# Linear attention with a routed feed-forward on one Trainium2 core: product groups of the attention loop run in pairs, with other PSUM banks

## What is computed

```python
xn = _layernorm(x)
qkv = xn @ W_qkv.T                                   # q, k, v by head
q_p = elu(einsum('bhnd,hdf->bhnf', q, proj)) + 1.0
k_p = elu(einsum('bhnd,hdf->bhnf', k, proj)) + 1.0
kv = einsum('bhnf,bhnd->bhfd', k_p, v)
attn = einsum('bhnf,bhfd->bhnd', q_p, kv)
z = 1.0 / (einsum('bhnf,bhf->bhn', q_p, k_p.sum(axis=2)) + 1e-08)
attn = (attn * z[..., None]) @ W_out.T + b_out
weights = softmax(where(logits >= second_best, logits, -inf))   # logits = xn @ Wr + br
ffn = sum over e of weights[e] * (gelu(xn @ W1[e] + b1[e]) @ W2[e] + b2[e])
out = x + attn + ffn
```

## Time and profile before

| | |
|---|---|
| median of 3 runs | 706.27 us (706.25 to 707.19) |
| profiled execution | 706.3 us |
| its span, first to last instruction | 704.2 us |
| TensorE, share of the span busy | 97% |
| VectorE, ScalarE | 73%, 68% |
| mean granted TensorE clock | 0.997 of full speed |
| HBM traffic | 94 GB/s over the span |

### The profile page before, as it was taken

How to read it: one execution, slowest core, us unless ns; L and a number is a source line. 1 busy time by engine, 2 the same in 40 slices (tenths; PEclk the granted TensorE clock), 3 DMA queues, 4 the chain that set the end, 5 groups by cost and what they waited for, 6 DMA issues and landing times.

```text
span 704.2 us, 17250 instructions
## 1 busy us (share of the span) xinstructions
PE 682.1 (97%) x5482; PEld 600.8 (85%) x5483; DVE 511.3 (73%) x1308; ACT 476.1 (68%) x875; POOL 227.5 (32%) x169
## 2 busy tenths in 40 slices
PE   8799999999999998999999999999999999999995
PEld 4666777777777776589999999999999999999995
DVE  8889989898989878847567674556776445577553
ACT  5687969696969696776477764457774444777551
POOL 1313232323242324633252332234223323313222
PEclk9999999999999999999999999999999999999998
DMA  8866474747474648856365563345636333554431
GB/s 262 197 183 169 108 226 105 226 106 226 106 226 105 196 105 230 232 169 187 58 105 170 80 165 46 52 65 93 188 60 171 51 47 67 87 150 60 58 46 22
DMA packets 87204, 91.63 MB, mean 130 GB/s; under 512 B 60049, under 2 KB 73361, under 8 KB 84897
## 3 DMA queue, kind: packets, MB, share of 16 engines
q1 hardware_dynamic: 71426, 59.36, 34.1%
q0 software_dynamic: 13872, 18.75, 15.2%
q10 hardware_dynamic: 1872, 13.11, 5.0%
HBM read 39.32 MB, written 26.67 MB: 94 GB/s over the span
## 4 chain that ended last, share of the span: by engine, by line
PE 79%; DVE 8%; issue 4%; SPq 3%; DMA 3%; ACT 2%; POOL 1%; POOLq 0%; DVEq 0%
PE F L502 9%; PE F L503 9%; PE F L504 9%; PE WK L502 5%; PE WK L504 4%; PE WK L503 4%; PE NUM L502 4%; PE NUM L504 4%; PE NUM L503 4%; PE DEN L574 4%; PE DEN L503 3%; PE DEN L502 3%; PE DEN L504 3%; PE F L565 3%; PE F L559 3%
## 5 line engine op out<-in xcount | busy, mean ns | idle before, releaser
L1864 POOL DMA_INDIRECT out<-ysb,icur x75 | 120.3, 1604 | 273.2 <-DVE ysb L1695 257.3
L1161 ACT ACTIVATE h<-F,b1c 128x384 f32<-128x384 f32 x200 | 112.2, 575 | 141.5 <-PE F L504 135.1
L1672 DVE TENSOR_TENSOR hl<-h,hh 128x768 fp32r<-128x768 f32 x100 | 95.9, 960 | 113.7 <-ACT hh L1165 113.7
L1015 ACT ACTIVATE e_ring<-F 128x512 f32<-128x512 f32 x256 | 145.6, 622 | 35.8 <-PE F L559 32.7
L502 PE MATMUL F<-gxh,wh 128*128 128x384 f32 (+1 forms) x400 | 129.1, 323 | 1.6 <-issue 1.1
L503 PE MATMUL F<-gxl,wh 128*128 128x384 f32 (+1 forms) x400 | 128.0, 320 | 0.0
L504 PE MATMUL F<-gxh,wl 128*128 128x384 f32 (+1 forms) x400 | 128.0, 320 | 0.0
L1798 POOL DMA_INDIRECT xg<-rows,slots x64 | 63.6, 994 | 175.3 <-PE F L559 142.2
L1405 DVE SCALAR_TENSOR_TENSOR kp<-F,e_ring 128x512 f32<-128x512 f32 x128 | 82.7, 681 | 12.4 <-PE DEN L574 6.2
L1405 DVE SCALAR_TENSOR_TENSOR qp<-F,e_ring 128x512 f32<-128x512 f32 x128 | 85.0, 685 | 5.8 <-ACT e_ring L1015 4.6
L1165 ACT ACTIVATE hh<-h 128x768 fp32r<-128x768 f32 x100 | 84.7, 847 | 3.3
(11 more groups left out here) (252 smaller groups left out, 1556.2 us busy)
## 6 DMA issues: line engine op xcount, KB each, us to landing
wraw<-experts ACTq DMA_DIRECT2D x12, 1024.0 KB, 6.7
gblk<-xg SPq DMA_DIRECT2D x100, 96.0 KB
Sk<-kdh SPq DMA_DIRECT2D x64, 128.0 KB, 2.4
Sq<-qdh SPq DMA_DIRECT2D x64, 128.0 KB
xin<-x SPq DMA_DIRECT2D x8, 512.0 KB
Sk<-kdl SPq DMA_DIRECT2D x32, 128.0 KB, 2.4
Sq<-qdl SPq DMA_DIRECT2D x32, 128.0 KB
xres<-x SPq DMA_DIRECT2D x8, 512.0 KB
```

Of the source, the lines that this page charges most:

```text
L1015: A(e_ring[:, u % 4, :], F[u % 4][:, :], ACT.Exp, bias=EXP_BIAS, scale=1.0 / DOWN).then_inc(exp_done, 1)
L1161: A(h32[:, m, :], F[m % 4][:, 0:T], ACT.Gelu, bias=b1c[:, w, m:m + 1]).then_inc(gelu, 1)
L1672: V.tensor_tensor(hl[:, 2 * q:2 * q + 2, :], h32[:, 2 * q:2 * q + 2, :], f32(hh[:, 2 * q:2 * q + 2, :]), ALU.subtract).then_inc(hl_rdy, 1)
L1864: pool.indirect_dma_start(out, bass.IndirectOffsetOnAxis(icur[:, s, :], 0), ysb[:, s, :], None, bounds_check=last_token, compute_op=ALU.ad ...
```

## The change

On PE, in iterations 0 to 6:
- `kv` 1 moves from behind unit 11 to directly behind `kv` 0; `kv` 2 moves from behind unit 17 to behind unit 18 and `qk_rest` 1, and `kv` 3 from behind unit 19 to directly behind it. Each second group waits for its features first.
- `attend` 1 moves from the end of the iteration, behind `project` 1, to directly behind `attend` 0 (unit 29). `attend` 2 moves from unit 0 of the next iteration to unit 1, directly ahead of `attend` 3.
- `prefix` moves from unit 30 to the iteration's end, behind `project` 1.
- `to_tokens` 1 waits for the first `tokens_lo`, and `tokens_T` 0 for the read of the positions.

In the final iteration, `attend` 2 and 3 of sequence 6 become a pair too; its other groups stay.

On ACT, the copies of the attended blocks follow their groups: 0 and 1 behind exp 29 (ahead of exp 30), 2 and 3 behind exp 1; `qk_lo` 3 moves from behind exp 29 to behind exp 30. On DVE, `numbers_of` moves from ahead of `residual` 1 to behind it.

Banks: x's first half from WK[0] to DEN, attended block 1 from WK[0] to DEN and block 3 from DEN to WK[0].

```diff
-    T_BANK = [WK[0], NUM]
+    T_BANK = [DEN, NUM]
-    ATT_BANK = [NUM, WK[0], WK[1], DEN]
+    ATT_BANK = [NUM, DEN, WK[1], WK[0]]
...
                 unit(b, u)
-                if u == 0 and not first:
-                    wait(pe, o_rdy, 2 * b - 1)
+                if u == 1 and not first:
+                    pe.wait_ge(o_rdy, 2 * b - 1)
                     attend(b - 1, 2)
-                if u == 1 and not first:
-                    pe.wait_ge(pos_read, b + 1)
+                    pe.wait_ge(qkl_rdy, 4 * b + 4)
                     attend(b - 1, 3)
                 if u == 2:
-                    if not first:
-                        pe.wait_ge(att_rdy, 4 * b - 2)
+                    pe.wait_ge(pos_read, b + 1)
                     tokens_T(b + 1, 0)
...
                     to_tokens(b - 1, 0)
+                    pe.wait_ge(xtl_rdy, 2 * b + 3)
                     to_tokens(b - 1, 1)
-                    pe.wait_ge(xtl_rdy, 2 * b + 3)
                     to_tokens(b - 1, 2)
...
                 if u == 10:
-                    if first:
-                        pe.wait_ge(pos_read, 1)
-                    else:
+                    if not first:
                         pe.wait_ge(at_rdy, 4 * b - 2)
                     kv(b, 0)
+                    pe.wait_ge(feat, 32 * b + 8)
+                    kv(b, 1)
                 if u == 11:
-                    kv(b, 1)
                     qk_rest(b + 1, 0)
...
-                if u == 17:
-                    kv(b, 2)
                 if u == 18:
                     qk_rest(b + 1, 1)
-                if u == 19:
+                    kv(b, 2)
+                    pe.wait_ge(feat, 32 * b + 16)
                     kv(b, 3)
...
                     attend(b, 0)
+                    attend(b, 1)
                 if u == 30:
                     qk_rest(b + 1, 3)
                     if not first:
                         project(b - 1, 0)
-                    prefix(b + 1)
                 if u == 31:
                     if not first:
                         pe.wait_ge(att_rdy, 4 * b + 1)
                         project(b - 1, 1)
-                    pe.wait_ge(qkl_rdy, 4 * b + 8)
-                    attend(b, 1)
+                    pe.wait_ge(att_rdy, 4 * b + 2)
+                    prefix(b + 1)
...
-                if u == 0 and not first:
-                    copy_att(b - 1, 1)
-                    copy_att(b - 1, 2)
                 if u == 1:
                     if not first:
+                        copy_att(b - 1, 2)
                         copy_att(b - 1, 3)
...
                 if u == 29:
+                    copy_att(b, 0)
+                    copy_att(b, 1)
+                if u == 30:
                     qk_lo(b + 1, 3)
-                    copy_att(b, 0)
...
-                if u == 31:
-                    numbers_of(b + 1)
...
                     if u == 31:
                         residual(b - 1, 1)
                 if u == 31:
+                    numbers_of(b + 1)
                     slots_of(b + 1)
```

More of the change, by code:

```diff
@@ L755, in final_iteration @@
                     keep_clock(NUM)
-                if u == 0:
+                if u == 1:
                     pe.wait_ge(o_rdy, 2 * b - 1)
                     attend(b - 1, 2)
-                if u == 1:
-                    pe.wait_ge(pos_read, b + 1)
+                    pe.wait_ge(qkl_rdy, 4 * b + 4)
                     attend(b - 1, 3)
```

## The result

The changed kernel took 717.43 us (median, 717.05 to 717.70), the kernel before 706.73 us beside it: ratio 1.015, interval 1.0134 to 1.0166. It is 10.7 us slower. The forecast was 713.7 us with a range of 708 to 717. The side was right. The sum had 7.4 us of loss, 3.3 us too few, and the time lies just above the range.

The account below looks back on a forecast made before the run. The prediction took a path alternating between PE, DVE and ACT as the bound, PE busy 97%. Terms of +0.66 and +0.58 us a period, with edge iterations, summed to 7.4 us: 706.3 + 7.4 = 713.7 us, range 708 to 717.

Parts of the forecast that it names:

- The switches: On PE, a second `attend` or `kv` group directly behind a first adds 0.88 us; each pair saves 0.32 us of PE.
- Attend 1 ahead of project: On PE between unit 27 and the end of `project` 1, `attend` 1 adds 0.88 us, as PE has no gap there.
- Q: The end of `project` 1 on PE, from which the forecast counted the times of the following steps.
- The turn on DVE: From `residual` 1 to `tokens_lo`, DVE and PE come together and 0.22 us is won back, net +0.66 us a period.
- kv 0 and 1: From the end of `kv` 0 to feature 14, the pair removes feature 14's 0.23 us of wait.
- kv 2 and 3 behind unit 18: From feature 14 to feature 21, exp 19 and its ACT queue come later: +0.58 us a period at feature 21, bounds 0.2 to 0.83.
- The sum over the loop: Over all iterations and turns: 3.3 + 3.5 + 0.3 - 0.1 + 0.4 = 7.4 us slower; period +1.24 us.
- the terms of the turn: Around the end of `project` 1: +0.88 us for `attend` 1, less 0.22 up to `tokens_lo`, net +0.66 us a period.
- PE stays the bound: Rival, chance 0.14: 28 pairs in iterations 0 to 6 save 0.32 us each, 9.0 us, giving 697.3 us.
- Only one term: Rival, chance 0.14: only the turn or only exp 19's queue costs, 3.6 or 3.8 us, about 710 us.
- Cancelling: Rival, chance 0.07: an earlier `products` 0 repays up to 0.3 us of each switch; saving and losses cancel, 706 us.

## Why the prediction was right and wrong

The path round the loop, cut at the steps that the forecast used. Each length is from one start in the timelines to the next:

| stretch | before | after | difference | forecast |
|---|---|---|---|---|
| feature 23's end to `residual` 1 | 8.71 | 9.41 | +0.70 | +0.88 |
| `residual` 1 to `tokens_lo` | 5.35 | 5.24 | -0.11 | -0.22 |
| `tokens_lo` to feature 8 | 6.69 | 6.66 | -0.03 | 0 |
| feature 8 to feature 14 | 4.58 | 4.35 | -0.23 | -0.23 |
| feature 14 to feature 21 | 7.35 | 8.69 | +1.34 | +0.81 |
| feature 21 to feature 23's end | 2.39 | 2.38 | -0.01 | 0 |
| sum | 35.07 | 36.73 | +1.66 | +1.24 |

- **The switches: right as lengths on the path.** A second group adds 0.86 us (attend) and a kv pair 1.88 (forecast 0.88 and 1.9), and two pairs of their own saved 0.56 us a period (forecast 0.32 each).
- **Attend 1 ahead of project: right place, 0.18 us too much.** The forecast left out that `prefix` goes from ahead of Q to behind it, and that unit 31 adds 0.23 us when it follows `project` 0 directly, and 0.34 behind `prefix`.
- **The turn on DVE: right place, 0.11 us too hopeful.** The forecast had DVE and PE arrive together. PE is last by 0.18 us. After its wait, `attend` 3 takes 1.06 us, where the working had a second group's 0.88, and the transposes of the first half add 0.59 us, where it had 0.45. DVE waited 0.98 and 0.32 us ahead of the residuals (forecast 1.0 and 0.5), and PE 0.91 us for feature 31 (0.9).
- **kv 0 and 1: right.** -0.23, and the kernel with this pair alone gave -0.23.
- **kv 2 and 3 behind unit 18: right place, the wrong size, and this is the step that failed.** Feature 14 to feature 21 grew by 1.34, not 0.81 us. Of the 0.53 us, unit 18 makes 0.28: it adds 0.51 us where the sum had 0.23. `to_heads` with `qk_group` 2 makes 0.18: from `to_heads`' start to `qk_hi` 2 it is 2.10 us for 1.92, and `to_heads` itself adds 0.66 for 0.44. The way from feature 14's start to unit 18 makes 0.09: 0.75 us, a feature's whole 0.70 and a hop of 0.05, for the 0.66 of the sum. The three are one mistake. The sum took the lengths from rows in which the engine streams, where an instruction begins before the one ahead is over and adds less than its own length. An instruction that had to be waited for adds its whole length, and this was to be seen before the change: in the chain of the kernel before, a query unit in the stream adds 0.24 us and unit 27, which waits for DVE, adds 0.50 (below). The Trainium skill (TensorE: Matmul & The Clock Gate, Single matmul latency) gives a lone matmul, there in bf16, a fixed part on top of its columns. The rows agree in kind, 0.51 us behind a wait against 0.23 in the stream.

```profile
151.30 0.50 PE F L565
...
154.83 0.24 PE F L565
```

- **The sum over the loop: the same term failed in iteration 0.** The term of kv 2 and 3 came to 1.34 - 0.23 = 1.11 us a period, not 0.58. Its bounds (0.2 to 0.83) were bounds of slack and didn't contain 1.11. The two profiled spans differ by 11.2 us, 3.8 more than the sum. Of these, iterations 1 to 6 make 2.5: 6 x 0.53 = 3.2 us too little for kv 2 and 3, less 0.7 us that the terms of the turn had too much. Without this luck the miss would have been larger. Another 1.1 us come from iteration 0 with its turn: the sum gave it 0.3 - 0.1 = 0.2 us, and the first `tokens_lo` behind it is 1.28 us later (61.40 for 60.12). `to_heads` is absent there, as the forecast said, but `v_copy` 0 stands behind exp 19 too: `qk_group` 2 waits 1.29 us for it, and feature 21 waits 1.59 us for exp 21 and starts 1.09 us later. The rest lies behind iteration 6. The two engines of the changed kernel, and feature 21 of the kernel before, in iteration 0:

```profile
44.45 0.50 PE L502 MATMUL WK<-xTh,WTh 128*128 128x512 f32 x1 [1.29 <-ACT vext L999]
```
```profile
47.27 1.41 DVE L1399 SCALAR_TENSOR_TENSOR qp<-F,e_ring 128x512 f32<-128x512 f32 x2 [1.59 <-ACT e_ring L1011]
```
```profile
46.18 1.28 DVE L1405 SCALAR_TENSOR_TENSOR qp<-F,e_ring 128x512 f32<-128x512 f32 x2
```

- **The rivals.** PE stays the bound (0.14): out, since PE's busy time fell and the time rose; so a saved switch alone doesn't set the time here. Only one term (0.14): out, both parts cost by themselves. Cancelling (0.07): out, the loss is 1.5%, clear of its interval.

## What to carry to other kernels

Putting two steps together saves a switch only where their engine holds the path at both old places; check for each moved step what the queue behind it feeds, since an engine that is 97% busy may still be waited on for one early result. When you add up a new chain, take the streamed length only for an instruction that follows another on its engine. For one that stands behind a wait, take its whole length. Look at everything that stands in the queue behind a late step, not only at the first step that waits for it. Work out the first iteration by itself, since other work is missing there. Find the place where a pair pays before giving it up: here the kv 0 and 1 pair where the change had it, and an attend pair at another place, gave 0.5%.

## What the runs showed of the hardware

The kernel before took 706.3 to 706.7 us beside three groups of runs and 718.2 to 718.8 us beside two others, steady within each, at a granted clock of 0.99 or more in all. At 718 us DVE stands 2.77 us ahead of feature 8 where it stood 0.86, with no releaser on the core. ACT stands 2.12 us at the same time, also with none, and PE has gaps in `kv` 1 that no wait explains. DVE, ACT and PE of the kernel before at 718 us:

```profile
180.51 0.69 DVE L1405 SCALAR_TENSOR_TENSOR kp<-F,e_ring 128x512 f32<-128x512 f32 x1 [2.77 <-remote]
```
```profile
180.55 0.60 ACT L1015 ACTIVATE e_ring<-F 128x512 f32<-128x512 f32 x1 [2.12 <-remote]
```
```profile
178.88 1.21 PE L574 MATMUL DEN<-kp,vext 128*32 128x128 f32 x16
180.38 0.68 PE L574 MATMUL DEN<-kp,vext 128*32 128x128 f32 x16 [0.29 <-issue]
```

The difference of the waits, 1.9 us, is about the growth of the period there, 1.7 us. The expectations say that PE lacks instructions there. That is only a name for gaps that no wait explains: no run tested it, and the cause stays open. The sets at 718 us and those at 706 us ran on different chips, and whether the chip is the cause wasn't tested either. It matters for tuning all the same: at 718 us the `kv` 0 and 1 pair gave nothing, at 706 us 0.2%, and the change itself cost 2.2% and not 1.5%. So the kernel before has to be timed beside each variant, and profiled there too.
